# The routed experts' results: gathered per token after the experts, or added to the tokens' rows in memory during them

## The reference, cut to what matters

```python
shared_out = _swiglu(xf @ shared_gate_up.T) @ shared_down.T
affinity = jax.nn.sigmoid(xf @ gate_w.T)
_, sel = jax.lax.top_k(affinity + expert_bias, 3)
sel_aff = jnp.take_along_axis(affinity, sel, axis=1)
gating = sel_aff / (sel_aff.sum(axis=-1, keepdims=True) + 1e-09)
hidden = _swiglu(jnp.einsum('td,efd->tef', xf, expert_gate_up))
expert_out = jnp.einsum('tef,edf->ted', hidden, expert_down)
routed_out = jnp.einsum('tk,tkd->td', gating, sel_out)      # sel_out: the 3 chosen of expert_out
x = x + shared_out + routed_out
```

## Time and profile before

| | us |
|---|---|
| runs | 1483.87, 1484.2, 1487.36 (median 1484.2) |
| profiled execution: its own time | 1478.98 |
| profiled execution: span of the profile | 1477.2 |
| PE busy | 1325.2 (90%) |
| DVE, ACT, POOL busy | 574.8, 466.2, 206.0 |
| mean granted clock of PE | 0.949 |

### The profile page before, as it was taken

The page is one execution under the profiler, slowest core; times in us unless marked ns, Lnnn a source line. Parts: engine busy times, 40 slices in busy tenths (PEclk is TensorE's granted clock), DMA queues, the critical chain, the costliest instruction groups (busy, mean ns, idle before and its releaser), DMA issues.

```text
span 1477.2 us, 17761 instructions
## 1 busy us (share of the span) xinstructions
PE 1325.2 (90%) x5796; PEld 836.1 (57%) x5797; DVE 574.8 (39%) x1546; ACT 466.2 (32%) x1008; POOL 206.0 (14%) x207
## 2 busy tenths in 40 slices
PE   4899999999998999899889999888399999669798
PEld 2554585565565554577557766655274676344476
DVE  9999632111234331111111111111573233556783
ACT  5899532222122100011111111111132232227783
POOL 1000000000000082000110010110732000102460
PEclk9999999999999999999999999999689899869899
DMA  9000000000201132511533124515540000200001
GB/s 239 32 1 1 2 2 0 1 1 0 86 29 64 51 87 90 200 44 37 212 135 114 43 74 169 212 34 201 135 158 1 1 1 1 93 0 0 1 29 43
DMA packets 45297, 96.92 MB, mean 66 GB/s; under 512 B 8495, under 2 KB 10857, under 8 KB 44065
## 3 DMA queue, kind: packets, MB, share of 16 engines
q1 hardware_dynamic: 27205, 68.70, 13.8%
q0 software_dynamic: 10560, 16.23, 4.1%
q10 hardware_dynamic: 7452, 10.97, 2.0%
HBM read 79.72 MB, written 16.10 MB: 65 GB/s over the span
## 4 chain that ended last, share of the span: by engine, by line
PE 76%; DVE 12%; issue 3%; DMA 3%; ACT 3%; POOL 1%; ACTq 1%; DVEq 1%; POOLq 0%
PE psum L416 38%; PE psum L1763 13%; PE psum L1818 7%; PE psum L1743 4%; PE psum L1937 3%; PE psum L1880 2%; PE psum L444 2%; DMA slot_outs<-sb_blk 1%; DVE sb_hT_conv L1366 1%; DMA sb_blk<-rows,sb_blk 1%; POOL sb_z_reg L611 1%; PE psum L1875 1%; ACT sb_htok L781 1%; PE psum L1843 1%; PE psum L1793 1%
## 5 line engine op out<-in xcount | busy, mean ns | idle before, releaser
L416 PE MATMUL psum<-sb_w_reg,sb_blk 128*128 128x256 f32 x896 | 210.3, 389 | 6.7 <-issue 6.7
L416 PEld LDWEIGHTS psum<-sb_w_reg,sb_blk 128*128 128x128 f32 x896 | 172.6, 196 | 40.4 <-issue 18.1
L1763 PE MATMUL psum<-sb_z_reg_r,sb_hT_conv_r 125*125 125x512 f32 x400 | 171.4, 429 | 0.2 <-issue 0.2
L416 PE MATMUL psum<-sb_w_reg,sb_hT_conv 128*125 128x512 f32 (+1 forms) x376 | 167.6, 595 | 0.9 <-ACT sb_hT_conv L1052 0.9
L1763 PE MATMUL psum<-sb_htok_r,sb_hT_conv_r 125*125 125x512 f32 x300 | 117.9, 393 | 0.0
L1162 DVE TENSOR_TENSOR sb_blk<-sb_blk,psum 128x256 f32<-128x256 f32 x56 | 23.6, 421 | 228.5 <-ACT sb_blk L755 228.5
L416 PEld LDWEIGHTS psum<-sb_w_reg,sb_hT_conv 128*125 128x125 f32 (+1 forms) x376 | 68.3, 188 | 77.4 <-issue 75.3
L1818 PE MATMUL psum<-sb_w_reg,sb_blk 128*128 128x512 f32 x224 | 108.2, 605 | 2.2
L416 PE MATMUL psum<-sb_hT_conv,sb_w_reg 128*128 128x416 f32 (+2 forms) x304 | 104.4, 504 | 1.6 <-ACT sb_hT_conv L450 1.6
L734 ACT CAST sb_hT_conv_r<-sb_a_reg 125x625 fp32r<-125x625 f32 x80 | 56.1, 715 | 115.0 <-PE psum L1763 114.9
L1763 PEld LDWEIGHTS psum<-sb_z_reg_r,sb_hT_conv_r 125*125 125x125 f32 x400 | 76.1, 190 | 25.7 <-issue 8.0
(11 more groups left out here) (375 smaller groups left out, 1746.4 us busy)
## 6 DMA issues: line engine op xcount, KB each, us to landing
sb_hT_conv<-w_expert SPq DMA_DIRECT2D x7, 2048.0 KB, 10.8
sb_w_reg<-w_expert SPq DMA_DIRECT2D x6, 2048.0 KB, 9.6
sb_hT_conv<-w_expert SPq DMA_DIRECT2D x7, 1024.0 KB, 12.8
slot_outs<-sb_blk ACTq DMA_DIRECT2D x28, 256.0 KB
sb_w_reg<-w_expert SPq DMA_DIRECT2D x6, 1024.0 KB, 12.5
sb_w_reg<-w_gnn SPq DMA_DIRECT2D x1, 4096.0 KB, 43.3
sb_w_reg<-w_qkv SPq DMA_DIRECT2D x1, 3072.0 KB, 20.1
slot_outs<-sb_blk ACTq DMA_DIRECT2D x1, 2560.0 KB, 10.5
```

Source lines behind the costliest of these rows:

```text
L416: ins = e.matmul(out, l, r, start=(n == 0), stop=(n == len(pairs) - 1))
L1763: ins = e.matmul(psum[0:TP, b, :], counts_at(l, 2 * i + n // NT)[:, s % HALF_T, :], z[s], start=(n == 0), stop=(n == len(pairs) - 1))
```

## The change

The results are no longer stored by slot and fetched by token. A second array in memory, `token_sums`, holds a row for each token (and 128 dummy rows that slots without a token point to). When VectorE has added the shared expert to a tile, ACT stores the tile of `x_res` there (ten plain stores, `sums_begun`). The list scattered to memory now has pairs (token, gate), 8 bytes in place of 4, with empty slots set to dummy rows; POOL reads it back in two layouts by eight DMAs in place of four, for blocks of 128 slots and for units of 32.

ACT multiplies each result by its gate as it copies it out of PSUM: `y_blk` for a whole block, and a column quarter of `y_units_a` or `y_units_b` for a unit. It issues no store. POOL adds the result to `token_sums` by an indirect transfer with `compute_op=ALU.add`: 128 rows of 512 for a whole block, 128 quarter rows of 128 for a unit. Two adds may never be under way together, since they may touch the same row, so each waits on `s_out` until the one before has landed. A whole block's add is issued by POOL one block later, behind the fetch for the block after; a turn's last whole block is added behind the first fetch in the next turn's whole blocks. The units' adds stand behind all the fetches of their stretch: first all fetches, then the adds of the last A expert's units, then those of the B expert's, then the next fetch. Fetches of units move 128 rows in place of 32. At the start a few adds of zeros to dummy rows take the place of results that don't exist yet.

After `stored`, SP loads `x_res` back by ten plain loads of a tile (125 partitions, 250 KB) each, and VectorE begins with the moments. The 30 fetches and the 30 additions are gone. SP issues the loads of `w_conv` and the others right behind the ten loads.

```diff
-        def pool_take(e, i):
-            for k in range(TOP_K):
-                n = i * TOP_K + k
-                r = n % NT
-                if n >= NT:
-                    e.wait_ge(take_added, n - NT + 1)
-                e.indirect_dma_start(ring[:, r, :], None, outs_dram,
-                    bass.IndirectOffsetOnAxis(ap=slot_i[:, k, i:i + 1], axis=0)).then_inc(ld_take[r], 16)
+        def pool_gather(e, g, unit):
+            e.wait_ge(s_xt, g + 1)
+            e.tensor_copy(idx, slot_tok[:, bass.ds(unit_of(e, unit), 1)]).then_inc(s_col, 1)
+            e.wait_ge(s_col, g + 1)
+            e.sem_inc(s_pass, 1)
+            e.indirect_dma_start(xg, None, rows_dram, bass.IndirectOffsetOnAxis(ap=idx, axis=0)).then_inc(s_row, 16)
+        def pool_add(e, n, done, unit):
+            e.wait_ge(s_y, done)
+            e.wait_ge(s_out, n * 16 + 16)
+            e.tensor_copy(to_idx, slot_tok[:, bass.ds(unit_of(e, unit), 1)]).then_inc(s_to_col, 2)
+            e.wait_ge(s_to_col, n * 2 + 2)
+            e.sem_inc(s_pass, 1)
+            e.indirect_dma_start(sums_dram, bass.IndirectOffsetOnAxis(ap=to_idx, axis=0), y_blk, None,
+                                 compute_op=ALU.add).then_inc(s_out, 16)
+        def pool_rest_gathers(e, rest, g, unit, behind):
+            with e.Fori(0, rest) as i:
+                last = (i + PER_BLOCK + 1 - rest) >> (PER_BLOCK.bit_length() - 1)
+                pool_gather(e, g + i + 1, unit + i + 1 + last * (behind - unit - rest))
+        def pool_rest_adds(e, rest, n, first, y, more=1):
+            with e.Fori(0, rest) as i:
+                e.wait_ge(s_y, n + i + more)
+                e.wait_ge(s_out, (n + i) * 16 + 16)
+                e.tensor_copy(to_idx, unit_row[:, bass.ds(unit_of(e, first + i), 1)]).then_inc(s_to_col, 1)
+                e.tensor_copy(y_unit, y[:, bass.ds(unit_col(e, i), 128)]).then_inc(s_to_col, 1)
+                e.wait_ge(s_to_col, (n + i) * 2 + 2)
+                e.sem_inc(s_pass, 1)
+                e.indirect_dma_start(sum_quarters, bass.IndirectOffsetOnAxis(ap=to_idx, axis=0), y_unit, None,
+                                     compute_op=ALU.add).then_inc(s_out, 16)
...
             with e.Fori(0, turns) as turn:
-                g, rest_b = block_at(e, turn), rest_of(e, T_B, turn)
-                pool_rest(e, rest_b, g, first_of(e, T_B, turn))
+                g, rest_b, first_b, first_a = block_at(e, turn), rest_of(e, T_B, turn), first_of(e, T_B, turn), first_of(e, T_A, turn)
+                pool_rest_gathers(e, rest_b, g, first_b, first_a)
+                e.wait_ge(sums_begun, NT * 16)
+                last_rest, last_added, last_unit = last_of(e, turn)
+                pool_rest_adds(e, last_rest, last_added, last_unit, y_units_a)
+                whole, rest_a, next_b = whole_of(e, turn), rest_of(e, T_A, turn), first_of(e, T_B, turn + 1)
+                pool_rest_adds(e, rest_b, g + 1, first_b, y_units_b)
                 g = g + rest_b
                 with e.Fori(0, whole) as i:
-                    e.wait_ge(s_xt, g + i + 1)
-                    pool_gather(e, g + i, unit + i * PER_BLOCK, SLOTS)
-                pool_rest(e, rest_a, g + whole, unit + whole * PER_BLOCK)
+                    pool_gather(e, g + i + 1, first_a + (i + 1) * PER_BLOCK)
+                    first = (16 - i) >> 4
+                    pool_add(e, g + i + 1, g + i + 1, first_a + i * PER_BLOCK - PER_BLOCK + first * (last_unit - first_a))
+                pool_rest_gathers(e, rest_a, g + whole, first_a + whole * PER_BLOCK, next_b)
+            last_rest, last_added, last_unit = last_of(e, turns)
+            pool_add(e, last_added, last_added + 1, last_unit - PER_BLOCK)
+            pool_rest_adds(e, last_rest, last_added + 1, last_unit, y_units_a, 0)
             with e.Fori(turns, end) as turn:
-                pool_rest(e, rest_of(e, T_B, turn), block_at(e, turn), first_of(e, T_B, turn))
+                g, rest_b, first_b = block_at(e, turn), rest_of(e, T_B, turn), first_of(e, T_B, turn)
+                pool_rest_gathers(e, rest_b, g, first_b, first_of(e, T_B, turn + 1))
+                pool_rest_adds(e, rest_b, g + 2, first_b, y_units_b, 0)
...
-            for i in range(NT):
-                pool_take(e, i)
...
         def act_block(e, g, unit):
...
-            e.wait_ge(s_out, g * 16 + 16)
-            e.copy(y_blk, psum[:, 5, :]).then_inc(s_y, 1)
-            e.wait_ge(s_y, g + 2)
-            e.dma_start(outs_dram[bass.ds(unit_of(e, unit) * UNIT, SLOTS), :], y_blk).then_inc(s_out, 16)
+            e.wait_ge(s_out, g * 16 + 48)
+            e.activation(y_blk, psum[:, 5, :], ACT.Copy, scale=slot_gate[:, bass.ds(unit_of(e, unit), 1)]).then_inc(s_y, 1)
...
+            for i in range(NT):
+                e.wait_ge(x_shared, i + 1)
+                e.dma_start(sums_dram[tile(i), :], x_res[:, i, :]).then_inc(sums_begun, 16)
...
+            e.wait_ge(stored, 1)
+            for i in range(NT):
+                e.dma_start(x_res[:, i, :], sums_dram[tile(i), :]).then_inc(ld_sums[i], 16)
...
-        def vec_taken(e, i):
...
+        def vec_summed(e, i):
+            if i >= 1:
+                vec_rstd(e, 2, i - 1)
+                vec_normed(e, 2, i - 1, htok[:, i - 1, :])
+            e.wait_ge(ld_sums[i], 16)
+            vec_moments(e, 2, i)
```

More of the change, by code:

```diff
@@ L500, in unit_of, with unit_col @@
                 skip_runtime_bounds_check_because="the experts' units are MAX_UNITS at most, and a dummy's behind them")
+        def unit_col(e, i):
+            return e.bass.s_assert_within(
+                i * 128, 0, (PER_BLOCK - 1) * 128,
+                skip_runtime_bounds_check_because="an expert has PER_BLOCK units at most behind its blocks")
         def from_table(e, column, turn, low, high):
@@ L667, in gpsimd @@
                 e.wait_ge(rows_stored[n], 16 * len(range(n, NT, 4)))
-            e.wait_ge(outs_filled, 16)
+            by_slot = list_dram.rearrange("(p c) o -> p (c o)", p=UNIT)
+            for j in range(PER_BLOCK):
+                part = slice(j * UNIT, (j + 1) * UNIT)
+                e.dma_start(slot_pairs[part].bitcast(I32), by_slot[:, 2 * j:2 * (j + SPANS)]).then_inc(s_idx, 16)
+            for j in range(PER_BLOCK):
+                part = slice(j * UNIT, (j + 1) * UNIT)
+                e.dma_start(unit_pairs[part].bitcast(I32), by_slot).then_inc(s_idx, 16)
+                e.memset(quarter[part], float(j)).then_inc(g_own, g_.up())
```

155 lines of the change are left out of this document (77 added, 78 removed).

## The result

The changed kernel takes 1537.9 us, median of 4 runs (1537.0 to 1544.2), where the kernel before takes 1484.0 beside it: ratio 1.037, 95% interval [1.034, 1.041]. The forecast was 1500, range 1486 to 1520: right in sign, 38 short. The profiled execution is the 1544.2 one, span 1542.3, so 65.1 over the span before; the medians differ by 54.

What follows compares the result with a forecast made beforehand. TensorE (PE) was taken as busy nine tenths of the span. 1479.0 - 12 + 10 + 13.6 + 4 = 1494.6 for the profiled execution; from the runs' median, 1484.2 + 15.6 = 1499.8, say 1500, range 1486 to 1520.

Steps and rivals of the forecast that it cites:

- Part 4: Whole blocks and the other turns of experts: net 4 us lost over the five changes, bounds 3 gained and 10 lost.
- Storing the ten tiles' sums from 567 to 603 lies under the shared expert's products: Before the experts: the stores of the sums are hidden, and the first fetch has 20 us to spare.
- the first turn's empty adds: At the experts' start: these adds end about when PE needs the next rows, costing 0, up to 3.
- the example: A two-unit turn change: next fetch moves from 761.02 to 775.9, rows land about 782.5, 3 us late.
- part 3: Four units between the fifth and sixth turn: serial adds make rows 11 late, restart 2.6; together 13.6, bounds 4 and 17.
- Part 2: Last unit, up to the last result S: dummy rows 7.4 late plus 2.3, say 10; bounds 6.5 and 16.
- Part 1: Tail: ten plain loads replace thirty fetches, QKV starts at S+18.6 in place of S+30.6; gain 12, bounds 10 and 16.
- the bound of 10: Tail: the gain is 10 in place of 12 if the filler runs wholly at the 1.2 GHz level.
- Whole blocks: Blocks stay 11.57 apart; an add that lands within 8.5 is covered, 28 times.
- the rival that made PoolE the bound: Whole blocks: a 256 KB add takes over 8.5; at 12 it costs 98, the rest making 1600; chance 0.10.
- Cover holds: Rival: adds land in about 3.3 even beside weights, but nothing is won; 1487, chance 0.13.
- faster: Rival: the hole behind S closes by 14 and a unit's add cycle stays within 4 us; 1478, chance 0.09.

Runs made afterwards that it cites:

- e1: Changed kernel with ScalarE's wait for the shared expert's products moved behind the loop of the ten stores of the sums; 1515.2 us, ratio 1.024.
- e11: e1 with units' fetches of 32 rows in place of 128, except the B experts' second and later units; 1508.8 us, ratio 1.019.
- e7: Changed kernel with units' indirect transfers that overwrite their rows' quarters in place of adding to them; 1521.3 us, ratio 1.026.
- e10: e9 with the last whole block's add ahead of the units' adds, and ScalarE's first block of a turn waiting for it alone; 1497.0 us, ratio 1.011.
- e8: Kernel before with only the tail changed: ten plain loads in place of thirty fetches and the products with gates; 1467.1 us, ratio 0.992.
- e14: e10 with units' fetches of 32 rows and the ten loads cut into 112 and 13 rows; 1486.4 us, ratio 1.0036.
- e9: e1 with the second whole block's fetch ahead of the units' adds and the dummy rows' fetch ahead of the last adds; 1522.9 us, ratio 1.028.
- e12: e10 with the last whole block's add in the turn before and A units' adds ahead of the second whole block's fetch; 1502.7 us, ratio 1.012.
- e15: e14 with the fetch of the second whole block's rows moved behind the A units' adds; 1499.9 us, ratio 1.012.
- e13: e12 with units' fetches of 32 rows and the ten loads cut into 112 and 13 rows; 1500.5 us, ratio 1.009.

## Why the prediction was wrong

- **Part 4, "Storing the ten tiles' sums from 567 to 603 lies under the shared expert's products", and "the first turn's empty adds ... 0, up to 3": this step failed.** It took each store to go when its tile is ready and didn't ask what stands ahead of the loop on ScalarE. Measured 25.6 by 634.0, of which e1 gives back 22.8 by moving one wait (21.1 counted from each kernel's first rows). The profiled execution is 49.6 above the prediction's sum for it (1544.2 against 1494.6), and this is half. The row that it should have been held against was at hand: ten such transfers are 22 us if nothing covers them. They took 31.5, the first of them beside the experts' weights.
- **Part 4, the changes: 4, bounds to 10; measured 16.3.** The mechanism (the next rows' fetch behind two serial adds) was right, and its length nearly so: the example has 14.9 from fetch to fetch (761.02 to 775.9), the trace 15.2 there (791.48 to 806.65), with landings of 6.7 to 8.3 for 7. The sum around it failed. It left out the cold restart, which part 3 has: 5.4. A unit follows the next 5.65 apart where it was 4.4 to 4.7, by e11 because of the wide fetch, priced at 0.4 a turn. And the table shows nothing of the 0.5 to 1.5 a turn that ScalarE was to give back. By e7 14 of the 16.3 is adding against writing; by e10 the order holds 8 of the 13.4 that e1 loses there.
- **Part 3: 13.6, bounds to 17; measured 20.4.** The working gave 14 late at the second block's rows, but the sum took 11, a value between it and one with landings of 3.3; measured 16.9 there (43.3 to 60.2), after 1.4 for the units' pace, and every add but the first and last landed in 7.1 to 8.5. The cold restart was right (2.1 against 2.6).
- **Part 2: 10, bounds to 16; measured 14.4.** The dummy rows came 11.0 later against 7.4: the whole block's add went out 7.8 behind the last unit's fetch (1084.08 to 1091.84), where I had 4.1, for by the chain it waits for the A unit's result, a wait in its helper's arguments that I left out; its landing, 4.73, and the way to the fetch, 4.3, were as taken. From the dummy rows to S it is 9.4 in place of 6.0, where I had 2.3 more.
- **Part 1: 12; measured 10.6**, and 11.9 in e8 (18.65 from issue to QKV). Right; the filler ran at the low clock in the profiled execution (8.31 against 7.29), the case that the bound of 10 named. Some luck is in it: behind the first tile VectorE set the pace (1.94 and 2.00 a tile), not the loads' 2.2, and the two happen to be close.
- **Whole blocks** stayed 11.57 apart, each add in 4.6 to 5.0 under its block: the rival that made PoolE the bound was rightly put low. *Cover holds* and *faster* assumed landings of 3.3 and less beside weights; measured 7.4 in the median there.

The terms make 25.6 + 16.3 + 20.4 + 14.4 - 10.6 = 66.1, and from QKV's start to the end 1.0 is won, which is within that stretch's noise: 65.1, the difference of the spans. That the medians differ by 54 and not by 65 is the two executions': one stands 5 under its kernel's median, the other 6 over.

What stays open: with e14's order the adds cost 17 up to the dummy rows (4.3 to 21.4), nearly all behind the four units, and 7.5 more from there to S (13.5, 6.0 before). What an execution's own drift adds to these two isn't separated. Double result buffers, or adds of one expert that don't wait for one another, weren't tried.

## What to carry to other kernels

A transfer "lies under" work only if the instruction that issues it does: read what stands ahead of it on its own engine, line by line, and price the whole batch in case the cover is missing. A serial chain of indirect transfers costs its length less its cover wherever it is put: before it is moved ahead of or behind a fetch, write down what waits behind it in either order (e9, e12 and e15 each mended one place and broke another), and send first what the earliest consumer needs.

## What the runs showed of the hardware

- With several plain DMAs under way on a queue, the issue of the next holds its engine. Ten stores of 125 rows took ScalarE 20.95, the first three 0.3 to 0.5 each and the last four 2.0 to 5.5; twenty of the same bytes in 112 and 13 rows took 9.83. The last of the ten landed 12.57 after its issue, so the engine is free well before the transfers are through.
- An indirect add of a unit costs PoolE 1.59 where the indirect write in its place costs 0.99 and a fetch of rows 1.0; an add of 16 bytes a row costs the same 1.59 as one of 512. The add lands 1.1 later than the write in the median. It lands in 3.3 to 3.4 alone, in 6.5 to 8.5 (median 7.4) beside full or nearly full DMA engines.
- A wider unit fetch (128 rows for 32) sets two units 0.9 further apart (5.7 against 4.8 in e1 and e11). Up to the dummy rows e11 kept 1.2 of it, where adds set the pace; e14 gained some 9 against e10 and e13 some 7 against e12, though each of these differences is of two executions. A price is seen only where nothing longer stands beside it.
- PE ran the block behind a wait for rows at a granted clock of 0.87, 12.9 for 11.57.
